# Four recurrence units of 16 value columns instead of eight of 8, with a new order of work on every engine

## What is computed

```
xa = ln(x);  sx = shift(xa) - xa;  xm_f = xa + sx*(maa_f + lowrank_f(xa + sx*maa_x)),  f = k,w,v,r,g
w = exp(-exp(time_decay + tanh(xw@td1)@td2));  r,k,v = three 512x512 projections;  g = silu(xg@Wg.T)
for t:  a = k_t (outer) v_t;  out_t = r_t . (u*a + s);  s = a + w_t*s        # s: 16x16 per head
x1 = x + groupnorm(out)*g @ Wo.T
xc = ln(x1), shifted and mixed to xk2, xr2;  y = x1 + sigmoid(xr2@Wfr.T)*(relu(xk2@Wfk.T)**2 @ Wfv.T)
```

## Time and profile before

| | |
|---|---|
| runs | 1888.52, 1889.99, 1893.34 us |
| profiled execution, its own time | 1890.35 us |
| its span in the trace | 1888.5 us |
| TensorE clock granted, mean | 0.977 of 2.4 GHz |
| instructions | 35795 |
| DMA | 181 MB, 96 GB/s over the span; 256 loads of vrep of 512 KB |

### The profile page before, as it was taken

One profiled execution on the slowest core, in us unless ns is written; L12 is line 12 of the kernel. 1 busy time (PEld: TensorE's weight loads), 2 busy tenths in 40 slices (PEclk: granted clock), 3 DMA queues, 4 the chain that ended last, 5 costly groups with the idle time before them and its releaser, 6 DMA issues.

```text
span 1888.5 us, 35795 instructions
## 1 busy us (share of the span) xinstructions
PE 1785.4 (95%) x12420; PEld 1235.2 (65%) x12420; DVE 1743.5 (92%) x2468; ACT 1174.2 (62%) x2945; POOL 1048.8 (56%) x886
## 2 busy tenths in 40 slices
PE   4788999999999999999999999999999999999855
PEld 2656667676666667666676776666677676667623
DVE  3499999999999999999999999999999999999871
ACT  3545666666666666666666666667666666766422
POOL 1235666556666655666665566665556665664531
PEclk8899999999999999999999999999999999999878
DMA  5233333333333343333333433333344333333310
GB/s 229 63 96 79 96 102 86 104 105 99 90 95 102 85 106 104 103 88 92 102 88 105 102 107 87 90 102 94 99 102 110 88 88 99 102 91 91 101 51 11
DMA packets 81601, 180.99 MB, mean 96 GB/s; under 512 B 18288, under 2 KB 34800, under 8 KB 80400
## 3 DMA queue, kind: packets, MB, share of 16 engines
q1 hardware_dynamic: 59920, 161.93, 32.2%
q10 hardware_dynamic: 21504, 16.78, 2.8%
HBM read 161.91 MB, written 16.78 MB: 95 GB/s over the span
## 4 chain that ended last, share of the span: by engine, by line
PE 49%; DVE 27%; issue 17%; DMA 3%; POOL 2%; ACT 1%; ACTq 0%; DVEq 0%; POOLq 0%; SPq 0%
PE bank L1088 17%; PE bank L1095 6%; DVE A L642 5%; PE bank L1133 5%; DVE S L657 5%; PE bank L1100 4%; DVE A L669 4%; PE bank L1213 3%; PE bank L1107 3%; DVE nmax L543 3%; DVE xf L600 3%; DMA vrep<-v_dram 3%; PE bank L1120 2%; DVE S L648 2%; PE bank L1169 2%
## 5 line engine op out<-in xcount | busy, mean ns | idle before, releaser
L466 POOL COPY S<-s 128x8 f32<-128x8 f32 x256 | 197.6, 773 | 321.9 <-DVE A L669 212.2
L657 DVE TENSOR_TENSOR_SCAN S<-wrep,S 128x512 f32<-128x512 f32 x256 | 354.5, 1385 | 0.7 <-ACT wrep L941 0.6
L669 DVE TENSOR_TENSOR A<-S,rt 128x1024 f32<-128x1024 f32 x256 | 330.9, 1293 | 0.1
L438 POOL TENSOR_TENSOR xf<-xf,xa 128x512 f32<-128x512 f32 x160 | 218.6, 1367 | 188.3 <-DVE xf L600 185.9
L642 DVE TENSOR_TENSOR A<-vrep,kt 128x1008 f32<-128x1008 f32 x256 | 309.6, 1210 | 10.2 <-DMA vrep<-v_dram 4.8
L857 ACT ACTIVATE prob<-bank,nmax 128x512 f32<-128x512 f32 x128 | 87.3, 685 | 249.0 <-DVE nmax L543 249.0
L648 DVE TENSOR_TENSOR S<-A 128x504 f32<-128x504 f32 x256 | 230.4, 910 | 1.2
L408 POOL TENSOR_SCALAR rstd<-mv 128x1 f32<-128x1 f32 (+1 forms) x96 | 71.7, 747 | 243.9 <-DVE mv L564 143.5
L410 POOL TENSOR_TENSOR hrs<-hrs,mhalf 128x32 f32<-128x32 f32 x32 | 200.5, 6266 | 2.7
L894 ACT ACTIVATE bank<-bank,par 128x128 f32<-128x128 f32 x640 | 174.9, 349 | 29.1 <-PE bank L1169 29.1
L1213 PE MATMUL bank<-A,slide 128*32 128x256 f32 x2048 | 166.2, 397 | 14.4 <-DVE A L669 14.4
(11 more groups left out here) (143 smaller groups left out, 3973.8 us busy)
## 6 DMA issues: line engine op xcount, KB each, us to landing
vrep<-v_dram SPq DMA_DIRECT2D x256, 512.0 KB
xc<-x_c SPq DMA_DIRECT2D x32, 256.0 KB, 6.3
xs<-x_s SPq DMA_DIRECT2D x32, 256.0 KB, 9.5
v_dram<-vT ACTq DMA_DIRECT2D x32, 256.0 KB, 7.3
out<-rr ACTq DMA_DIRECT2D x32, 256.0 KB, 6.2
Wv<-big_w SPq DMA_DIRECT2D x1, 1024.0 KB, 6.2
Wk<-big_w SPq DMA_DIRECT2D x1, 1024.0 KB, 8.2
Wr<-big_w SPq DMA_DIRECT2D x1, 1024.0 KB, 10.2
```

The costliest lines, as they stand in the source:

```text
L438: po.tensor_tensor(xf[:, b, :, :], xf[:, b, :, :], xa[:, :, 1:P + 1], ALU.add).then_inc(pool_mid.sem, 1)
L466: po.tensor_copy(S[:, u % 2, :, 0], s0[:, p, k:k + UJ]).then_inc(pool_wkv.sem, 1)
L657: ve_.tensor_tensor_scan(s, wrep[:, u % C, :, :].rearrange("p j t -> p (j t)"), s, 0.0, ALU.mult, ALU.add).then_inc(dve_scan.sem, 1)
L669: ve_.tensor_tensor(out4, s, r, ALU.mult).then_inc(dve_read.sem, 1)
```

## The change

One unit now covers a chunk with all 16 value columns (UJ = 16, U = 4). `vrep` and S have one buffer, A keeps two (of twice the size). The scan still works on 512 columns (WJ = 8), twice per unit, over the same `wrep`. The PE sum has 512 columns. The second low-rank transpose takes columns 64 to 160 (96 of them), so that g's part stands on partitions 64 to 95. xx shares memory with xhat, kk with xk2, pv with rk2. `head_u` is computed by ACT. x of batch 0 is loaded first, and Wv has a semaphore of its own. Waits on constants that hold anyway are dropped. All orders are new: steps have six lags (37 steps), and DVE, POOL and ACT handle each stage one step index later than before for most of their pieces, while PE keeps its lags but for G.

```diff
-UJ = 8
-U = C * HS // UJ
+UJ = 16
+U = C
+WJ = 8
-CONSTS = 14 + C
-LAGS = 5
+CONSTS = 14
+LAGS = 6
 FRONT_JOBS:
-    "O:1 V:0 Tx:1 W1:1 Mn:0 Wt:1 Mm:0 Mv:1 Mw:1 S0:0 S1:0 S2:0 Vp:1 Mk:1 Mr:1 Mg:1 D1:1 S3:0 Kp:1 "
-    "D2:1 E2:1 Rp:1 T0:0 T1:0 T2:0 G:1 T3:0").split())]
+    "G:2 V:0 Tx:1 Mn:0 Mm:0 W1:1 S0:0 Wt:1 S1:0 Mv:1 Mw:1 S2:0 S3:0 D1:1 Mk:1 Mr:1 Mg:1 Vp:1 T0:0 "
+    "T1:0 T2:0 T3:0 O:0 Kp:1 D2:1 E2:1 Rp:1").split())]
-        wrep = sb("wrep", [P, C, UJ, T2])
+        wrep = sb("wrep", [P, C, WJ, T2])
-        vrep = sb("vrep", [P, 2, UJ, P])
+        vrep = sb("vrep", [P, UJ, P])
-        S = sb("S", [P, 2, UJ, T2])
+        S = sb("S", [P, UJ, T2])
+        xx = by_chunk(xhat[:, :])
+        kk = xk2
+        pv = rk2
# SP: load_vrep
-                v1 = held(sp, regs[1], dve_outer.count(f"a{(u - 2) % U}", n if u >= 2 else n - 1))
+                v1 = held(sp, regs[1], dve_outer.count(f"a{(u - 1) % U}", n if u >= 1 else n - 1))
-                sp.dma_start(vrep[:, u % 2, :, :].rearrange("p j t -> p (j t)"),
-                             src[c][:, j0 * P:(j0 + UJ) * P].unsqueeze(1).broadcast_to([HC, HS, UJ * P]))\
-                    .then_inc(vrep_loaded[u % 2], 16)
+                sp.dma_start(vrep[:, :, :].rearrange("p j t -> p (j t)"),
+                             src[u].unsqueeze(1).broadcast_to([HC, HS, UJ * P])).then_inc(vrep_loaded, 16)
# SP: step, new order
+                load_x(b1+1)  load_s0(b1)  load_st0(b3)  load_vrep(b2,0)  load_vrep(b2,1)  load_st1(b0)
+                load_vrep(b2,2)  load_vrep(b2,3)
# POOL: wkv_s0
-                v1 = held(eng, regs[1], dve_read.count(f"q{(u - 2) % U}", n if u >= 2 else n - 1))
+                v1 = held(eng, regs[1], dve_read.count(f"q{(u - 1) % U}", n if u >= 1 else n - 1))
-                po.tensor_copy(S[:, u % 2, :, 0], s0[:, p, k:k + UJ]).then_inc(pool_wkv.sem, 1)
+                po.tensor_copy(S[:, :, 0], s0[:, p, HS * u:HS * (u + 1)]).then_inc(pool_wkv.sem, 1)
# DVE: wkv_pair also waits for the read before; wkv_scan
+                eng.wait_ge(dve_read.sem, dve_read.count(f"q{(u - 1) % U}", n if u else n - 1))
+                for j in range(0, UJ, WJ):
+                    s = S[:, j:j + WJ, :].rearrange("p j t -> p (j t)")
+                    last = ve_.tensor_tensor_scan(s, w, s, 0.0, ALU.mult, ALU.add)
# PE: wkv_sum
-                    last = pe.matmul(bank[SUM_BANK][32 * g:32 * g + 32, 2 * P * half:2 * P * (half + 1)],
-                                     ones, A[:, u % 2, g:UJ:4, :], start=(c == 0), stop=(c == C - 1))
+                    last = pe.matmul(bank[SUM_BANK][32 * g:32 * g + 32, :], ones, A[:, u % 2, g:UJ:4, :],
+                                     start=(u == 0), stop=(u == C - 1))
# PE: mid_Wt
-                pe.transpose(bank_of("Wt")[0:2 * DM, P:2 * P], txn[:, P - DM:P + DM], ident[:, :]).then_inc(pe_mid.sem, 1)
+                pe.transpose(bank_of("Wt")[0:3 * DM, P:2 * P], txn[:, 2 * DM:5 * DM], ident[:, :]).then_inc(pe_mid.sem, 1)
```

More of the change, by code:

```diff
@@ L202, in col @@
             return par[:, k:k + 1]
-        setup_loaded = [sem(f"setup_loaded{i}") for i in range(3)]
+        setup_loaded = [sem(f"setup_loaded{i}") for i in range(4)]
         x_loaded = [sem(f"x_loaded{i}") for i in range(2)]
@@ L209, in build @@
         st0_loaded = [sem(f"st0_loaded{i}") for i in range(2)]
-        vrep_loaded = [sem(f"vrep_loaded{i}") for i in range(2)]
+        vrep_loaded = sem("vrep_loaded")
         v_stored = sem("v_stored")
@@ L221, in units @@
             return " ".join(f"{x}{u}" for u in range(U) for x in text.split())
-        dve_att = Steps(sem("dve_att"), "stats aggr nm mx0 mx1 mx2 ri1 ri0 mx3 ri2 ri3 xin xst xag nm1")
-        dve_mid = Steps(sem("dve_mid"), "sx xx s0m mv mw mk mr mg s0c g")
+        dve_att = Steps(sem("dve_att"), "stats aggr nm mx0 mx1 mx2 ri1 ri0 ri2 mx3 ri3 xin xst xag nm1")
+        dve_mid = Steps(sem("dve_mid"), "sx xx mv mw mk mr mg s0m s0c g")
         dve_pre = Steps(sem("dve_pre"), "kw rw")
@@ new lines, in step @@
+                if b5: fin_y(*b5)
+                if b3: wkv_pair(*b3, 2)
+                if b2: mid_mix(*b2, 3)
+                if b2: mid_mix(*b2, 4)
+                if b4: tail_gn(*b4)
+                if b3: wkv_scan(*b3, 2)
+                if b4: tail_gate(*b4)
+                if b3: wkv_outer(*b3, 3)
+                if b3: wkv_read(*b3, 2)
+                if b4: tail_x1(*b4)
+                if b4: tail_st(*b4)
+                if b1: att_xin(*b1)
+                if b4: tail_ag(*b4)
@@ L830, in _ @@
             eng.wait_ge(setup_loaded[0], 32)
+            eng.wait_ge(pool_const, CONSTS)
+            for c in range(C):
+                sc.activation(head_u[:, c, :], head_rep[:, :], ACT.Copy, scale=col("u", c)).then_inc(act_setup, 1)
             def att_norm(n, m, p, i):
@@ L886, in mid_txt @@
                 sc.activation(tx[:, :], bank_of("Wt")[:, 0:P], ACT.Copy)
[L887 removed]
+                sc.activation(txg[2 * DM:3 * DM, :], bank_of("Wt")[2 * DM:3 * DM, P:2 * P], ACT.Copy).then_inc(act_mid.sem, 1)
             def mid_bias(n, m, p, f):
@@ new lines, in step @@
+                if b2: mid_bias(*b2, "g")
+                if b1: att_scale(*b1, 3)
+                if b2: mid_v(*b2)
+                if b1: att_probT(*b1, 0)
+                if b1: att_probT(*b1, 1)
+                if b1: att_probT(*b1, 2)
+                if b1: att_probT(*b1, 3)
+                if b4: tail_oT(*b4)
+                if b4: tail_xhat(*b4)
+                if b2: mid_ez(*b2)
+                if b2: mid_k(*b2)
+                if b2: mid_w(*b2)
+                if b4: tail_xc2(*b4, 0)
```

378 lines of the change are left out of this document (154 added, 224 removed).

## The result

Changed kernel: median 2155.29 us of 4 runs (2149.02 to 2158.89); kernel before, measured beside it: 1890.28 of 4. Ratio 1.140, 95% interval 1.137 to 1.143. The forecast was 1866 with a range up to 1930: wrong sign, and outside the range. The profiled execution took 2153.69 us, its span is 2152.0.

What follows compares the result with a forecast made beforehand. DVE and PE, both nearly full, were taken to bound the step. Terms -0.72 - 0.8 + 0.7 + 0 gave -0.8 us, times 31 steps -25, with start and drain -24: 1890.35 to 1866 us; range 1848 to 1884, whole 1832 to 1930.

Steps and rivals of the forecast that it cites:

- The reload: Loading vrep into its single buffer between outer products: 7.9 us, DVE waits 0.9, net 0 per step (bounds 0 and +2.7).
- The middle: Reload time of 7.9 us, taken between 9.3 at the old load's rate and 6.5 at the weights' rate.
- The credit: POOL's stalls of DVE, some 0.9 us, fall into the reload wait, making its net cost 0.
- the stretches of 8.9 and 7.0 us: DVE's work between outer 1 and outer 2 (8.9) and between outer 2 and outer 3 (7.0), set against the reload.
- Rival A: Reload keeps its old rate, 1.8 us more per step before outer 3: 1927 us; 35% with what goes like it.
- Port stalls: DVE waiting inside instructions for the port shared with POOL: -0.8 us of 4.2 per step (bounds -1.6 and 0).
- The wait for the means: DVE waits on POOL for the means after `tail_rstd` moves close behind `tail_ag`: +0.7 us per step (0.3 to 1.6).
- Fixed cost: DVE's outer, pair and read half as many: 12 instructions fewer at 0.06 us each, -0.72 us per step.
- PE's sum: PE's sums of 512 columns: 4 x 1.0 against 8 x 0.58 us, -0.6, PE's busy time 53.9 per step.
- Start and drain: Start: x loaded first and head_u off POOL, -2.4 us; drain: last batch's three uncovered reloads, +3 (0 to +8).
- no batch's path got longer: LAGS 6 adds a step in name only, since every DVE piece moved one step down.
- the terms without the reload: Whole sum with the reload at net 0: 31 steps of -0.8 make -25, with start and drain -24 us.

Runs made afterwards that it cites:

- sp_order: Changed kernel with SP's load of vrep for unit 0 put ahead of the loads of s0 and st0: 2065.31 us, ratio 1.094.
- sp_x: Changed kernel with unit 0's vrep load ahead of s0 and st0, and next batch's x loaded behind it, one step earlier: 2037.25 us, ratio 1.078.
- small_load: Changed kernel loading only 2 of vrep's 16 value columns per reload, same waits, v's values left out: 1869.67 us, ratio 0.990.
- heads16: Changed kernel with each vrep reload cut into eight DMAs, one per head, so on 16 engines: 1979.43 us, ratio 1.048.
- halves_moved: Changed kernel with SP's vrep and x loads reordered, vrep as two half buffers, outer 3 behind read 2 on DVE: 1877.59 us, ratio 0.993.
- before_no_add: Kernel before with POOL's five additions of xa cut from 512 to 4 columns: 1870.03 us, ratio 0.989.
- distinct_rows: Changed kernel with each vrep reload fetching 1 MB of 128 different weight rows, on 16 engines, v left out: 1868.42 us, ratio 0.988.
- before_one_vrep: Kernel before with one vrep buffer of 8 columns in place of two: 2434.47 us, ratio 1.289.

## Why the prediction was wrong, step by step

**The reload (failed step).** "I take the middle, 7.9: wait 0.9 ... Net 0 (bounds 0 and +2.7)" measured +8.4 us per step. This is the step of the prediction that failed: the size of the reload of vrep, and with it the wait in front of the outer product. Five things were missing or mis-sized in one term:

- Rate. The middle leaned on the weights' row. Packets of the replicated load took 9.1 to 9.5 us, above even the 7.8 that twice the old row gives. Rivals and range both ended at 9.3 for the whole reload; without any queue it is 11.6.
- The end. 0.85 us lie between the last packet and the instruction that waits.
- The queue. Load 0 stands behind s0's wait for z3 in SP's order: 3.4 us more. Worth 90 us by sp_order. The step that was moved was on SP, and no sentence of the prediction had followed it.
- The neighbour. x's 512 KB go out on the same engines behind load 3: 28 us by sp_x.
- The credit. 0.9 us of stalls were to fall into the wait of outer 3. It came to 0.4 (the gate takes 1.20 us on the mean where it takes 1.60 in small_load; the scans stay at 3.6).

Take the queue and the neighbour out, and 167 us are left (2037 to 1870): the length of the reload.

By the measured lengths the stretches of 8.9 and 7.0 us that the forecast worked out give 11.6 - 8.9 = 2.7 and 12.7 - 7.0 = 5.7 for outer 2 and 3. Measured are 2.7 and 3.7: the first is right, the second is too long by 2, since the stretch holds 2.0 us more than was counted: the scans take 1.2 more than undisturbed ones, the gate 0.5 more, and 0.35 are idle time in front of the gate. The method of setting the transfer's chain against the work between two users was right, only its entries weren't. It was set up for two of the four reloads, though; the two stretches across the batch's border, the longest by work but with the late issue, were never looked at, and outer 0 has 2.1 us of the 8.4.

**Rival A** ("the reload keeps its rate, 1927") had the mechanism and too small a price: its own sign, "over 1.5 us a batch in front of" the outer product, came in at 8.4. The forecast said that a step of over 56 would be none of its cases. The step is 63.3 in the stretch shown.

**The rate per engine, and what stands around the packets.** The Trainium skill, "DMA: Bandwidth & Descriptors", Specifications, gives some 27 GiB/s per engine, by which 1 MB on 8 engines would take 4.5 us. Measured were 9.1 to 9.5 on 8 engines, or some 14 GB/s each; the measurement decides. The same page, Rules for kernel authors, says that an outermost dimension smaller than 16, a broadcast of a few copies for instance, keeps a DMA to that many engines. The trace agrees on the number (8 packets of 4 B per load), but heads16 shows that for this source 16 engines were worth 1.2 times as much as 8. The same page's section on the anatomy of a DMA, which is about DMAs issued from GpSimd, puts most of the fixed cost behind the last byte, since the semaphore waits for the confirmed write. These loads are issued by SP, and the trace has it otherwise: 1.4 us ahead of the first packet, 0.85 behind the last.

**Port stalls, -0.8.** Measured 0. The excess of DVE's instructions over their undisturbed length was 4.69 us per step before, 4.74 in small_load and 4.82 in halves_moved. Pairs (2.06 before) and reads (0.64) lost theirs; the low-rank input (`mid_xx`, L575, 1.07), the means (0.98) and the gate (0.92) took them over. Two rows of small_load show it:

```profile
1040.53 1.60 DVE L698 TENSOR_TENSOR ogT<-ogT,gT 128x512 f32<-128x512 f32 x1
...
1051.33 1.14 DVE L511 SCALAR_TENSOR_TENSOR nmr<-mv,rstd 128x1 f32<-128x1 f32 x1 [0.46 <-POOL rstd L405]
```

The gate is 0.68 undisturbed and took 1.60, and an operation of one column took 1.14. The changed kernel has the same, beside the add of POOL that runs meanwhile:

```profile
1027.71 1.18 POOL L431 TENSOR_TENSOR xf<-xf,xa 128x512 f32<-128x512 f32 x1
...
1027.78 1.14 DVE L510 SCALAR_TENSOR_TENSOR nmr<-mv,rstd 128x1 f32<-128x1 f32 x1 [0.46 <-POOL rstd L404]
```

Six DVE instructions a step are longer than undisturbed by over 0.15 us in the kernel before, and six in small_load: fewer borders between instructions did not mean fewer meetings. before_no_add is the other side of it: with the adds cut the excess fell to 1.93.

**The wait for the means, +0.7.** Its idle time went from 0.47 to 0.61 us per step, +0.14, though the same operation is stretched by 0.98 as above, which stands in the stalls.

**Fixed cost, -0.72.** Right. From start to start the outer product is 2.17 us for two of 1.12, the read 2.20 for two of 1.13, the pair 1.12 for two of 0.59.

**PE's sum, 1.0 instead of 2 x 0.58.** Right. The first records of the sum and of what follows it in the changed kernel:

```profile
1050.85 1.06 PE L1180 MATMUL bank<-A,slide 128*32 128x512 f32 x8
1051.84 1.16 PE L1137 MATMUL bank<-tx,w 32*128 32x128 f32 x16
```

It is 0.99 us. The window of a step of small_load, where nothing waits for vrep, has PE busy for 53.20 us (the forecast: 53.9) and DVE for 53.80. The step is 54.6, not the 54.0 of the forecast:

```profile
1000.00:1054.60 54.60, 53.20 (x358) 37.41 (x358) 53.80 (x66) 36.18 (x94) 29.69 (x24) 1.00 0.10 31
```

**Start and drain, -2.4 and +3.** The gate's instructions, one per batch, in small_load (min, median, max ns; first and last start):

```profile
L698 DVE TENSOR_TENSOR ogT<-ogT,gT x32: 661/1598/1603, 167.3 to 1839.1; 128x512 f32<-128x512 f32 x32
```

In the kernel before the same instruction ran from 165.9 to 1857.4. The first comes 1.4 us later here (2.1 earlier in distinct_rows, 163.8), so the -2.4 isn't borne out. Batch 0 is ahead by 2.2 us when its mixing begins (`mid_shift` at 42.5 us in the changed kernel, at 44.7 before), but its first outer product comes at 80.0 for 74.2: "no batch's path got longer" did not hold for that one.

The 31 intervals from there are 19.7 us shorter together: the last three 10.5 (143.2 us for 153.7), the first four 2.9, the 24 steady ones 0.26 each, 6.3. That wider units shorten the chain of a batch that has the chip to itself would fit the last three, but it isn't shown. In the changed kernel, with the waits for vrep, the last three take 158.8 us, 5.1 more than before: the drain's +3 (0 to +8) had the right sign and range, as the sum of a gain it didn't know and a larger loss.

So the terms without the reload, -24 in the forecast, came to -18 in small_load with other parts: -9 in the steps for -25, and -9 at the ends for +0.6, of which the +3 was for reloads that small_load hardly has.

## What to carry to other kernels

A buffer that is refilled in a loop costs the whole chain from the end of its reader to the start of the next: the queue ahead of the issue, the issue, the first packet, the packets at the rate of this very access pattern, and the time from the last packet to the waiting instruction. Set it against the shortest stretch between any two users, for each of them, the border between batches too; if it is longer, two half buffers of the same bytes can do (2155 to 1891 us here by themselves, to 1878 with the orders of SP and DVE mended too). Take the rate from a transfer that reads the same way, not from the fastest one with rows of the same length; and before giving a gain for fewer instructions beside a second engine on the same port, find which instruction the stall will meet next.

## What the hardware showed that was not expected

- Rows read by 16 partitions each came at 110 GB/s on 8 engines and 133 on 16; different rows in the same place of the kernel at 282, weights at the start at some 400.
- The replicated load's rows of 8192 B moved slower than rows of 4096 B: 110 GB/s against 121 to 131, 9.1 to 9.5 us per MB against 4.0 to 4.2 per half (before_one_vrep, halves_moved).
- 0.85 us, on average, from a load's last packet to the start of the instruction waiting for it.
- A DVE operation of 128x1 took 1.14 us instead of 0.16 while POOL's add ran.
- TensorE's mean granted clock was 0.977 before, 0.934 in the changed kernel and 0.894 in before_one_vrep, where PE is busy for 95, 86 and 80% of the span: the less it was busy, the lower.

**Left open:** why replicated rows come slowly, and why longer ones come slower still; what another order on POOL would do to the 4.7 us of stalls, which nothing in the change touched (not tried); two full buffers of vrep in the changed kernel (not tried).
